# Layer norms applied on ScalarE with per-token scale and shift, smaller stages and another order of work, in a decoder layer on one core

## The reference

```python
x = _layernorm(x + attn(x, ...))          # bit-linear qkv, 16 heads, chunks of 128 tokens, softmax + recurrent kv state, RMS norm, bit-linear proj
x = _layernorm(x + xattn(x, ctx, ...))    # 32 heads on 8 kv heads, keys from x and from ctx, window of 64, ALiBi bias, Wo
x = _layernorm(x + ffn(x, ...))           # base linear + router over 8 experts (top 2) with LoRA of rank 16
def _layernorm(x, axis=-1, eps=1e-05):
    m = jnp.mean(x, axis=axis, keepdims=True)
    v = jnp.var(x, axis=axis, keepdims=True)
    return (x - m) / jnp.sqrt(v + eps)
```

## Time and profile before

| | before |
|---|---|
| median of 3 runs (lowest to highest) | 1296.49 us (1296.21 to 1297.39) |
| the profiled execution, its own time | 1297.64 us |
| its span, first to last instruction | 1295.5 us |
| TensorE busy | 923.4 us, 71% |
| VectorE busy | 551.9 us, 43% |
| ScalarE busy | 286.3 us, 22% |
| GpSimd busy | 87.0 us, 7% |
| mean granted TensorE clock | 0.81 of full speed |

### The profile page before, as it was taken

The page is one execution under the profiler, slowest core; times in us unless marked ns, Lnnn a source line. Parts: engine busy times, 40 slices in busy tenths (PEclk is TensorE's granted clock), DMA queues, the critical chain, the costliest instruction groups (busy, mean ns, idle before and its releaser), DMA issues.

```text
span 1295.5 us, 23211 instructions
## 1 busy us (share of the span) xinstructions
PE 923.4 (71%) x10038; PEld 604.3 (47%) x10038; DVE 551.9 (43%) x1105; ACT 286.3 (22%) x549; POOL 87.0 (7%) x103
## 2 busy tenths in 40 slices
PE   2555865867687777867777867778767876778575
PEld 2342753356434653356433754356533664355323
DVE  3425145442644346443644247443545336132322
ACT  4112212412042111412032211401132210411220
POOL 0101001010001001010001001010000100000001
PEclk9756886988888867988778877988779787888686
DMA  9501000000000000000000000000000000000000
GB/s 315 137 2 33 2 1 1 1 33 2 17 1 34 2 1 17 2 34 2 1 17 26 9 2 17 1 34 2 2 17 17 1 2 17 2 1 1 17 1 17
DMA packets 18818, 27.15 MB, mean 21 GB/s; under 512 B 5401, under 2 KB 7577, under 8 KB 18721
## 3 DMA queue, kind: packets, MB, share of 16 engines
q1 hardware_dynamic: 18432, 24.84, 6.1%
q10 hardware_dynamic: 288, 0.80, 0.2%
HBM read 21.44 MB, written 4.19 MB: 20 GB/s over the span
## 4 chain that ended last, share of the span: by engine, by line
PE 41%; issue 30%; DVE 18%; ACT 7%; POOL 2%; DMA 2%; DVEq 0%; POOLq 0%; SPq 0%; ACTq 0%
PE ps L859 9%; DVE max_b L1181 4%; PE ps L899 4%; PE ps L869 3%; ACT p_b L648 2%; PE ps L879 2%; PE ps L832 2%; PE ps L776 2%; PE ps L805 2%; PE ps L808 2%; PE ps L932 2%; PE ps L796 2%; PE ps L964 1%; ACT p_a L599 1%; DVE x L1157 1%
## 5 line engine op out<-in xcount | busy, mean ns | idle before, releaser
L1181 DVE TENSOR_REDUCE max_b<-ps 128x4 f32<-128x768 f32 (+2 forms) x160 | 105.7, 711 | 128.8 <-PE ps L913 67.7
L899 PE MATMUL ps<-k_b,q_b 32*128 32x192 f32 (+2 forms) x1024 | 77.3, 432 | 104.5 <-DVE max_b L1181 84.3
L648 ACT ACTIVATE p_b<-ps 128x512 f32<-128x512 f32 (+1 forms) x256 | 118.5, 549 | 123.7 <-PE ps L941 123.7
L899 PEld LDWEIGHTS ps<-k_b,q_b 32*128 32x128 f32 x1024 | 54.4, 249 | 129.2 <-DVE max_b L1181 95.5
L932 PE MATMUL ps<-q_b,k_b 32*128 32x512 f32 (+1 forms) x512 | 76.8, 674 | 32.9 <-ACT p_b L648 31.3
L1066 DVE SCALAR_TENSOR_TENSOR nat<-ps,st_a,qkv_bias 128x512 f32<-128x512 f32 x48 | 35.6, 746 | 115.8 <-PE ps L729 115.8
L964 PE MATMUL ps<-wo,o_fb 128*128 128x512 f32 x128 | 68.4, 695 | 20.5 <-DVE o_fb L1218 20.5
L859 PE MATMUL ps<-c_t,wq 128*128 128x256 f32 x256 | 70.8, 439 | 6.7 <-ACT wq L570 6.7
L1003 PE MATMUL ps<-base_t,x_t 128*128 128x512 f32 x128 | 73.5, 706 | 0.0
L957 PE MATMUL ps<-p_b,v_b 128*32 128x256 f32 (+1 forms) x1024 | 66.1, 379 | 2.4 <-ACT p_b L648 2.4
L859 PE MATMUL ps<-x_t,wq 128*128 128x256 f32 x256 | 66.2, 416 | 0.0
(11 more groups left out here) (174 smaller groups left out, 1545.1 us busy)
## 6 DMA issues: line engine op xcount, KB each, us to landing
x_in<-x SPq DMA_DIRECT2D x8, 512.0 KB, 3.7
c_in<-ctx SPq DMA_DIRECT2D x8, 512.0 KB, 4.4
y<-x SPq DMA_DIRECT2D x8, 512.0 KB, 2.8
p_b<-L_attn_qkv_w SPq DMA_DIRECT2D x3, 1024.0 KB, 7.2
p_b<-L_xattn_Wq SPq DMA_DIRECT2D x1, 2048.0 KB, 10.8
p_b<-L_attn_proj_w SPq DMA_DIRECT2D x1, 1024.0 KB, 9.7
p_b<-L_ffn_base_w SPq DMA_DIRECT2D x1, 1024.0 KB, 8.9
wo<-L_xattn_Wo SPq DMA_DIRECT2D x8, 128.0 KB, 8.9
```

Source lines behind the costliest of these rows:

```text
L648: act.activation(p_b[:, j % 2, s, 0:cols], bank(4 + s)[:, 0:cols], ACT.Exp, scale=DB ** -0.5).then_inc(pb_here.sem, 1)
L899: pe.matmul(bank(4 + r)[:, (i % 2) * N:(i % 2) * N + 2 * n * S], q_b[strip[r], i, :, :].rearrange("p h q -> p (h q)"), k_b[strip[r], half, ...
L1181: ins = dve.tensor_reduce(max_b[:, half, 0, i:i + k, 2 * n:2 * n + 2], ps[:, 4 + 2 * n:6 + 2 * n, :].rearrange("p r (i n) -> p i r n", i=2 ...
```

## The change

Five kinds of edit, and nothing of what is computed:

1. `norm_apply` goes from VectorE to ScalarE. VectorE now only works out a shift, -mean * rstd, for both tiles in one small instruction (`norm_shift`), and ScalarE does z * scale + shift with both as per-token operands, one instruction for each tile, for all three norms.
2. Three more pieces change engine: the copy of the kv state (`a1_state`) and that of V (`b1_v`) go from VectorE to ScalarE, both roundings from VectorE (one instruction of 1024 columns) to GpSimd (two of 512, right behind the scaling).
3. Stages are cut smaller, so that other work can stand between the pieces: `b2` on VectorE by pair and bank pair, `b3` into `b3`, `b3_on` and `b3_of`, `b1_k` by source, `a1_state` into `a1_qt` and `a1_state`, the recurrent product out of `a2_v` (`a2_rec`), `c2` into `c2_z`, `c2` and `c2_y`, `b1_q` by any range of k.
4. All lists are reordered. `b4`, the last exponentials `b3`(7) and `b1_c`'s copies on ScalarE, and the second and third of `a1_qkv`(1, ...) move over the step's border to the head of the next step. The product with Wo now stands ahead of `b1_q`, `a1_qt` and `c1_x2`.
5. The context's load is issued one step earlier.

```diff
-            run(sp, [(NEXT, a0), (A, b1), (C_, c2)], late)
+            run(sp, [(NEXT, a0), (C_, c2), (NEXT, b1)], late)
...
             def a0(b):
...
+                for t in range(T):
+                    ins = pool.tensor_scalar(xq[:, t, :], y_a[:, t, :], MAGIC, MAGIC, ALU.add, ALU.subtract)
+                ins.then_inc(x_round.sem, 1)
...
+            def norm_apply(z, rs, row, dst, t):
+                return act.activation(dst[:, t, :], z[:, t, :], ACT.Identity, scale=rs[:, row + 1, t:t + 1], bias=rs[:, row + 2, t:t + 1])
+            def b4_x2(b, t):
+                    sh_here(act, b)
+                    y_sent.before(act, b)
+                    norm_apply(x1, rs_b, 0, x2, t).then_inc(x2_here.sem, 1)
...
-            def norm_apply(b, z, mv, rs, row, rstd, dst, done):
-
+            def norm_shift(b, mv, rs, row, rstd, done):
                 rstd(dve, b)
-                for t in range(T):
-                    ins = dve.tensor_scalar(dst[:, t, :], z[:, t, :], mv[:, t, 0:1], rs[:, row + 1, t:t + 1], ALU.subtract, ALU.mult)
-                    if done.per == T or t == T - 1:
-                        ins.then_inc(done.sem, 1)
+                dve.scalar_tensor_tensor(rs[:, row + 2, :], mv[:, :, 0], -1.0, rs[:, row + 1, :], ALU.mult, ALU.mult).then_inc(done.sem, 1)
...
-            run(pe, [(C_, c1_x2), (B, of(b1_q, 0, range(KT))), (B, b1_x1), (C_, c1), (B, of(b1_q, 1, range(KT))),
+            run(pe, [(A, of(a1_qkv, 1, [1])), (A, of(a1_qkv, 1, [2])), (C_, of(b4, 1, 0)), (C_, of(b4, 0, 0)), (C_, of(b4, 0, 1)),
+                     (C_, of(b4, 1, 1)), (B, of(b1_q, 0, range(2))), (B, of(b1_q, 0, range(2, KT))), (A, a1_qt), (C_, c1_x2), (C_, c1),
+                     (B, of(b1_q, 1, range(2))), (B, b1_x1), (B, of(b1_q, 0, range(KT, 6))), (A, a1_state), (B, of(b1_q, 1, range(2, KT))),
+                     (A, of(a1_v, 0)), (B, of(b1_k, 0)), (A, of(a1_v, 1)), (B, of(b1_k, 1)), (A, of(a2_s, 0, range(HT))), (B, b1_v),
```

More of the change, by code:

```diff
@@ L514, in a3 @@
                 ins.then_inc(o_scaled.sem, 1)
+                o_scaled(pool, b)
+                xq_turn(pool, b)
+                carried(pool, "pool")
+                for t in range(T):
+                    ins = pool.tensor_scalar(xq[:, t, :], y_a[:, t, :], MAGIC, MAGIC, ALU.add, ALU.subtract)
+                ins.then_inc(o_round.sem, 1)
             def a4(b):
@@ L578, in a1, with a1_state @@
                                bankb(0).rearrange("p (t k n) -> p t k n", t=T, k=KT), ACT.Copy).then_inc(xq_here.sem, 1)
+            def a1_state(b):
+                kv_full(act, b)
+                for s in range(HT):
+                    ins = act.activation(kv_bd[s * S:(s + 1) * S, :, s * S:(s + 1) * S],
+                                          bank(0)[s * S:(s + 1) * S, :].rearrange("p (k n) -> p k n", k=KT)[:, :, s * S:(s + 1) * S], ACT.Copy)
+                ins.then_inc(kv_here.sem, 1)
             def a1_q(b):
@@ L649, in b3, with c1_x2 @@
                                    scale=DB ** -0.5).then_inc(pb_here.sem, 1)
-            def c1_x2(b):
-                for t in range(T):
+            def c1_x2(b, t):
                     x2_turn(act, b, t + 1)
@@ L666, in _ @@
             of = lambda f, *n: lambda b: f(b, *n)
-            run(act, [(C_, c1_x2), (B, b1_x1), (C_, c1), (A, a1_q), (A, a1_v),
-                      (A, of(a2_m, 0)), (B, b1_k), (A, of(a2_x, 0, range(HT))), (B, of(b1_q, 0)), (A, of(a3_sq, 0)),
-                      (A, of(a2_m, 1)), (A, of(a2_x, 1, range(HT))), (B, of(b1_q, 1)), (A, of(a3_sq, 1)),
-                      (B, of(b2, 0)), (C_, c2), (A, a3_t), (B, of(b2, 1)),
-                      (B, of(b3, 0)), (B, of(b3, 1)), (NEXT, a1), (B, of(b3, 2)), (B, of(b3, 3)), (B, of(b3, 4)), (B, of(b3, 5)),
-                      (B, of(b3, 6)), (B, of(b3, 7)), (A, b1_c)], late, mix)
+            run(act, [(C_, of(b3, 7)), (B, of(b1_c, 0)), (B, of(b1_c, 1)), (C_, of(b4_x2, 0)), (C_, of(b4_x2, 1)), (C_, of(c1_x2, 0)),
+                      (C_, of(c1_x2, 1)), (B, of(a4, 0)), (B, of(a4, 1)), (C_, c1), (B, of(b1_x1, 0)), (B, of(b1_x1, 1)), (A, a1_q),
+                      (A, a1_state), (A, a1_v), (A, of(a2_m, 0)), (A, of(a2_x, 0, range(HT))), (B, of(b1_q, 0)), (A, of(a3_sq, 0)),
+                      (B, b1_k), (B, of(b1_q, 1)), (B, b1_v), (A, of(a2_m, 1)), (A, of(a2_x, 1, range(HT))), (A, of(a3_sq, 1)),
+                      (B, of(b2, 0)), (C_, c2), (A, a3_t), (B, of(b2, 1)), (B, of(b3, 0)), (NEXT, a1), (B, of(b3, 1)), (B, of(b3, 2)),
+                      (B, of(b3, 3)), (C_, c2_y), (B, of(b3, 4)), (B, of(b3, 5)), (B, of(b3, 6))], late, mix)
         @block.tensor
@@ L1167, in a4, with b2 @@
             def a4(b):
-                x2_here.before(dve, b)
-                norm_apply(b, out_a, mv_a, rs_a, 2, ra_here, x1, x1_here)
-            def b1_v(b):
-                v_full(dve, b)
-                dve.tensor_copy(v_b[:, :, :, 0:DB], bank(7).rearrange("p (j g d) -> p j g d", j=KB, g=KVB)).then_inc(v_here.sem, 1)
-            def b2(b, half, pair):
-                for n in range(2):
+                norm_shift(b, mv_a, rs_a, 2, ra_here, sa_here)
+            def b2(b, half, pair, n):
                     sb_full(dve, b, 8 * half + 2 * pair + n + 1)
@@ L1198, in b2_max, with b3_on @@
                     c.end()
+            half = G * QB // 2
             def b3(b, r):
+                if r:
+                    on_here(dve, b, 1)
+                pv_done(dve, b, KB * r + KB)
+                for n in range(2):
+                    ins = dve.transpose(o_nat[:, n * half:(n + 1) * half, :], bank(2 + n).rearrange("p (x q) -> p x q", q=S))
+                ins.then_inc(ob_read.sem, 1)
+            def b3_on(b, r):
                 c = ch["b3"]
@@ L1203, in b3 @@
                     c.start(dve, b)
-                else:
-                    on_here(dve, b, 1)
-                pv_done(dve, b, KB * r + KB)
-                half = G * QB // 2
-                for n in range(2):
-                    ins = dve.transpose(o_nat[:, n * half:(n + 1) * half, :], bank(2 + n).rearrange("p (x q) -> p x q", q=S))
-                ins.then_inc(ob_read.sem, 1)
                 ob_read(dve, b, r + 1)
@@ L1215, in b3, with b3_of @@
                 if r:
-                    on_here(dve, b)
-                    for n in range(2):
+                    c.end()
+            def b3_of(b, n):
+                        on_here(dve, b)
                         dve.transpose(o_fb[:, 2 * n:2 * n + 2, :].rearrange("p h (i q) -> p (h i) q", q=S),
                                       on_b[:, n * half:(n + 1) * half, :]).then_inc(of_here.sem, 1)
-                    c.end()
             def b4_z(b, t):
```

146 lines of the change are left out of this document (83 added, 63 removed).

## The result

The changed kernel took 1064.1 us (median of 4 runs, 1063.7 to 1070.7), beside 1296.4 us for the kernel before on the same chip (1293.2 to 1297.4): a ratio of 0.822, 95% interval 0.819 to 0.826. The prediction was 1138 us with a range down to 1095. The direction was right, and so was what the gain is made of (less idle time, less low clock); the gain was 232 us and not 158.

A forecast was written before the change was run, and what follows sets the result against it. TensorE's work plus its idle time, with low clock behind waits, was taken as the bound. Six steps: 110 idle - 24 hand-offs + 58 clock = 144; with 11 + 6 - 2 outside, 159 us, giving 1138 us, range 1095 to 1205.

The forecast's parts named there:

- clock term: Six full steps: only the score loops run at low clock, costing 42 us against 100 before, a gain of 58 us.
- score loops: TensorE's waits around the score pairs, mostly for VectorE's maxima: 69.0 us before, 48.6 left in six steps, gain 20.4.
- the prediction's formula: Low clock's cost in TensorE's work: busy time at the low level times (1 - 1/1.8), about 0.44.
- no low clock and no losses: Rival for the whole kernel: gains of 210 us in six steps and 20 outside, giving 1066 us; chance 0.06.
- 24 us for hand-offs: Six full steps: small hand-offs the walk leaves out, charged at 4 us a step, 24 us off the gain.
- walk: Stage-by-stage pass through the new lists with measured durations, estimating what TensorE still waits for in each full step.
- border: Step's border, around Wo and x2's transposes: TensorE's waits fall from 47.2 to 11.7 us in six steps, gain 35.5.
- last loop: Last loop's score blocks waiting for exponentials: 21.1 us before, 17.4 left in six steps (about 2.9 each), gain 3.7.
- The turn: Loop's turn, ahead of `a1_qkv` after the change: taken as 0, other end 20 us; as a rival, 1158 us, chance 0.10.
- The sign named in the prediction: A gap over 1 us ahead of the first `a1_qkv` in steps 3 to 6 but not 7 would be the turn.
- Step 1 and the end: Outside the six steps: step 1 gains 11 us, steps 8 and 9 gain 6, step 0 and the tail lose 2.
- The norm's engine: Norm of x2: 0.76 us a tile on ScalarE against 1.22 on VectorE, about 0.5 us a tile won on the chain.

## Why the prediction was wrong, step by step

It said 159 us and the spans of the two profiled executions differ by 232.8. The 73.8 us lie as follows: 47.1 in the six steps (191.1 against 144), 12.7 in step 1 (23.7 against 11), 9.0 behind them (15.0 against 6), 5.0 at the start (the start of step 1 came 3.0 us earlier, where 2 were to be lost). Of the 47.1 us in the six steps, 34 are clock (92.4 against 58) and 12.5 idle time (98.7 against the 86.2 that are left of 110.2 behind the 24 for hand-offs).

**The clock term failed: 58 us forecast, 92 measured.** The step was: "the two score loops are where TensorE still stands often. I take these as low and the rest at full clock". Measured, the clock is low for 6.8 us a step, 5.7 of them in the score loops, and not for 24. The rows of step 4 above show the score loops at 1.00 but for one dip behind a wait of 2.1 us; its waits of 1.35, 1.25 and 1.07 us left the clock up (in step 2 one of 1.35 did not). To size the cost: without the loop the clock is 0.98, low for 4% of the time, which by the prediction's formula costs 0.04 x 566 x 0.44 = 10 us, so the work is worth 556 us at 2.4 GHz (an estimate). The low clock then cost 110 us before (forecast 100), and 17 are left (forecast 42). The prediction gave no row for a whole region at the low level. Of its own rows from a score loop, 771.5 stands at 0.57, but 787.5, in the second half of the same step's score blocks, at 1.00. The rival "no low clock and no losses", 1066 us, came nearest and had got a chance of 0.06. Its 2 us from the measured time are luck: it put 210 us in the six steps and 20 outside, measured are 191.1 and 41.7.

**The 24 us for hand-offs did not exist.** The walk itself was good. Idle time left in the six steps, the waits of after grouped as the walk was:

| place | forecast left | measured | rows |
|---|---|---|---|
| border | 11.7 | 12.3 | L903 <- x, L1009, L1030 |
| router, kv state | 6.3 | 7.4 | L903 <- x_t, L786 |
| first attention | 17.7 | 15.7 | L828, L815, L837 |
| score loops | 48.6 | 42.2 | L944, L965, L849, L977 <- maxt_b |
| last loop | 17.4 | 26.5 | L977 <- p_b, L1002 |
| turn (with 1.6 of small gaps) | 0 | 12.2 | L771 <- issue |
| small waits and hand-offs | 28.8 | 1.7 | the rest |
| sum | 130.5 | 118.0 | |

The five places that were walked sum to 104.1 against 101.7. In the score loops the wait behind `a2_out`(1) was 2.25 in the walk and is 2.10, those of the second half were 1.25, 1.4, 0.9 and 0.2 and are 1.25, 1.35, 1.07 and 0.26; only the first `b2_max` was far out, 1.1 and 0.21 (all in step 4). In the last loop the waits for the exponentials were under-priced: 4.4 us a step and not 2.9. A flat allowance on top of a walk with measured durations was a second charge for the same thing.

**The turn was priced at 0 and costs.** The sign named in the prediction came true to the letter: a gap over 1 us ahead of the first `a1_qkv` at 343.7, 458.1, 574.6 and 691.9 us, and none at 804.1. Its own size, 14 us by the kernel without the loop, lies within the two ends given, 0 and 20. This error went the other way, so the two above were larger than the sum shows. (The Trainium skill, "Runtime: NRT & Kernel Launch", Instruction fetch mechanics, has a taken branch outside the fetched pages stall for a fetch. By that rule the gap should be there, and the trace agrees; that a fetch is its cause no run here separates.)

**Step 1 and the end were sized by guess.** In step 1 idle fell from 44.7 to 24.6 us, by 20.1. Of these, 3.9 are the wait for the mixed weights, which ended at 128.1 us and now ends at 121.2 (the start of step 1 at 124.0 cuts it in two, so step 1 and the start are hard to part). The other 16.2 are as much as a full step gains in idle time (16.5), and not under half: nearly all of the walk's places are there without C_. Behind step 7 idle fell by 3.4 us, and work by 11.6, as the clock rose from 0.77 to 0.88: that part had no clock term at all.

**Right**: that TensorE's idle time and clock set the time; that the border's wait goes by what stands behind Wo (31 us when it is uncovered); that the score loops resist longest (L944 is still the first row, and 42.2 us are left there, though 26.8 went); that the roundings on GpSimd are hidden, although at 1.92 us each and not 0.695. Of the profile it foretold, TensorE's share (83% of a step, foretold 82), the longest wait for the maxima (2.10 us, behind `a2_out`(1)), the missing wait for q's copy and that of x2's transposes came; the clock (0.97, foretold 0.90) did not.

**The norm's engine** was read wrongly, at no cost in time. ScalarE's norm was taken at 0.76 us and takes 0.81, hidden. The 1.22 us set against it were VectorE's beside GpSimd's sum; alone VectorE takes 0.54. So the half us a tile comes from the sum, beside which VectorE slows down and ScalarE does not (0.81 us too in the kernel before with its norms on ScalarE). (The Trainium skill, "ScalarE: Activation LUTs", Rules for kernel authors, would keep adds and multiplies on VectorE. For the single instruction the rows agree, 0.54 against 0.81, and the prediction's "does not agree" holds only beside the sum. With the norm back on VectorE the time of the changed kernel is the same, so here it decides nothing either way.)
